# Depthwise and pointwise convolution in jobs of 784 pixels on four corners of the matrix engine, half of the ninth products summed by GpSimd, and a ratio by a scalar operand

## What is computed

```
x = x + L0(_gn(x))      # _gn: group norm over pairs of channels, eps 1e-5
x = x + L1(_gn(x))
L0(x): h = sign(x); h = depthwise 3x3 conv(h, sign(dw)); h = bn1(prelu(h)); h = sign(h)
       h = einsum('bchw,oc->bohw', h, sign(pw)); h = bn2(prelu(h)); return h + x
L1(x): filters = einsum('bchw,oc->bohw', x, W) + b        # 9 filter planes per channel
       return sum over the 9 taps k of (x shifted by tap k) * filters_k
```

## Time and profile before

| what | value |
|---|---|
| median of 3 runs | 834.75 us |
| the profiled execution | 835.78 us |
| its span, first to last instruction | 833.9 us |
| busy: VectorE (DVE) | 747.3 us, 90% |
| busy: TensorE (PE) | 702.7 us, 84% |
| busy: GpSimd (POOL) | 573.4 us, 69% |
| busy: ScalarE (ACT) | 518.5 us, 62% |

### The profile page before, as it was taken

One profiled execution on the slowest core, in us unless ns is written; L12 is line 12 of the kernel. 1 busy time (PEld: TensorE's weight loads), 2 busy tenths in 40 slices (PEclk: granted clock), 3 DMA queues, 4 the chain that ended last, 5 costly groups with the idle time before them and its releaser, 6 DMA issues.

```text
span 833.9 us, 19099 instructions
## 1 busy us (share of the span) xinstructions
PE 702.7 (84%) x7975; PEld 404.2 (48%) x7975; DVE 747.3 (90%) x1136; ACT 518.5 (62%) x772; POOL 573.4 (69%) x393
## 2 busy tenths in 40 slices
PE   0766889899998989998999989998999989897783
PEld 0323556455555555554555555554555555552221
DVE  6211799999999999999999999999999999999998
ACT  4586876667676767667685767766675767633000
POOL 2000167878787787878687786878787777778885
PEclk9988999999999999999999999999999999999986
DMA  5101559798887979698888889697988888686983
GB/s 205 44 1 31 140 115 248 149 210 192 173 219 160 235 147 246 139 233 170 210 182 173 215 163 247 140 238 159 217 180 171 212 172 165 142 174 143 198 165 95
DMA packets 40023, 142.14 MB, mean 170 GB/s; under 512 B 5248, under 2 KB 13440, under 8 KB 37888
## 3 DMA queue, kind: packets, MB, share of 16 engines
q0 software_dynamic: 17296, 75.87, 50.7%
q1 hardware_dynamic: 22640, 65.04, 23.4%
HBM read 25.86 MB, written 25.69 MB: 62 GB/s over the span
## 4 chain that ended last, share of the span: by engine, by line
DVE 56%; PE 32%; issue 6%; ACT 5%; DMA 1%; SPq 0%; DVEq 0%
DVE prod L685 35%; PE tap_ps L356 18%; PE dw_ps L369 11%; DVE prod L697 7%; DVE tap_ps L685 6%; DVE xb L659 4%; PE pw_ps L390 2%; ACT ab L416 2%; DVE st L651 1%; ACT unused L416 1%; PE pw_ps L381 1%; DVE st L555 1%; DMA prod<-prod 1%; ACT signs L416 1%; DVE prod L705 0%
## 5 line engine op out<-in xcount | busy, mean ns | idle before, releaser
L356 PE MATMUL tap_ps<-q,w_t 64*64 64x392 f32 x2304 | 466.9, 500 | 63.6 <-DVE prod L697 61.3
L356 PE MATMUL tap_ps<-mirror,w_t 64*64 64x392 f32 x2304 | 479.9, 517 | 0.0
L685 DVE SCALAR_TENSOR_TENSOR prod<-tap_ps,bias,q 128x784 f32<-128x784 f32 x448 | 452.3, 1029 | 11.5 <-PE tap_ps L356 7.3
L369 PE MATMUL dw_ps<-signs,dw_diag 64*64 64x392 bf16 x2304 | 246.3, 335 | 16.0 <-ACT ab L416 13.6
L416 ACT ACTIVATE ab<-dw_ps,col 128x392 bf16<-128x392 f32 x256 | 158.5, 669 | 160.0 <-PE dw_ps L369 160.0
L356 PEld LDWEIGHTS tap_ps<-q,w_t 64*64 64x64 f32 x2304 | 171.8, 134 | 166.9 <-DVE prod L697 95.8
L369 PEld LDWEIGHTS dw_ps<-signs,dw_diag 64*64 64x64 bf16 x2304 | 146.3, 108 | 139.2 <-issue 81.4
L282 POOL TENSOR_TENSOR prod<-prod 128x784 f32<-128x784 f32 x63 | 117.0, 1857 | 90.3 <-DVE prod L697 90.3
L289 POOL TENSOR_TENSOR prod<-prod 128x784 f32<-128x784 f32 x63 | 139.7, 2218 | 27.6 <-DMA prod<-prod 27.6
L356 PEld LDWEIGHTS tap_ps<-mirror,w_t 64*64 64x64 f32 x2304 | 124.6, 133 | 2.2
L304 POOL TENSOR_TENSOR ob<-prod 128x784 f32<-128x784 f32 x63 | 116.8, 1854 | 10.6 <-POOL prod L295 10.3
(11 more groups left out here) (101 smaller groups left out, 464.2 us busy)
## 6 DMA issues: line engine op xcount, KB each, us to landing
prod<-prod POOLq DMA_DIRECT2D x63, 1176.0 KB, 10.3
xb<-in_x_dram SPq DMA_DIRECT2D x16, 1568.0 KB, 11.7
out_dram<-ob SPq DMA_DIRECT2D x64, 392.0 KB, 2.9
mirror<-q SPq DMA_DIRECT2D x128, 101.5 KB, 4.6
prod<-prod SPq DMA_DIRECT2D x1, 146.2 KB, 2.3
prod<-in_L_conv_W_dram SPq DMA_DIRECT2D x1, 144.0 KB, 6.3
prod<-prod SPq DMA_DIRECT2D x1, 20.8 KB, 6.1
prod<-in_L_conv_prelu_a_dram SPq DMA_DIRECT2D x1, 0.2 KB, 2.3
```

The costliest lines, as they stand in the source:

```text
L356: mm = pe.matmul(rows3(tap_ps[to, u % SLOTS, side, 0:CH]), w_t[own, k, :], moving, start=True, stop=True)
L369: mm = pe.matmul(rows3(dw_ps[own, 0:CH]), dw_diag[own, k, own], signs[own, c * ROWS + dy:c * ROWS + dy + ROWS, dx:dx + WD], start=(k == 0) ...
L685: v.scalar_tensor_tensor(place.rearrange("p j (a b) -> p j a b", b=WD), psum.rearrange("p j (a b) -> p j a b", b=WD), s_(t, B4) if k == 4 ...
```

## The change

- L0 goes in 4 jobs of 784 pixels instead of 8 chunks of 392. `depthwise` has 36 matmuls a job, on all four corners: a corner's input rows are the image, its output columns the chunk. Signs, ReLU and `x1_sum` take 784 elements in one instruction. One buffer `conv_ps` (two banks) serves the depthwise result and then the pointwise one, so the next job's `depthwise` waits for this job's `x1_sum`. Jobs start at 20 + 9j.
- In odd quarters the ninth product is written to a ninth plane; there `pair` is left out. ScalarE adds the mean to that plane (`add_mean`) and GpSimd adds it (`add68`).
- `ratio` uses `tensor_scalar` with a per-partition scalar in place of `tensor_tensor`.
- x is kept in 3 buffers instead of 4, `signs` in 2 instead of 1. Many positions are moved.

```diff
-        xb = sb("xb", [P, RING, NPIX], F32)
-        signs = sb("signs", [P, HP, WP], BF16)
+        xb = sb("xb", [P, X_RING, NPIX], F32)          # X_RING = 3
+        signs = sb("signs", [P, 2, HP, WP], BF16)
-        dw_ps = ctx.enter_context(nc.psum_tensor("dw_ps", [P, 512], F32))
-        pw_ps = ctx.enter_context(nc.psum_tensor("pw_ps", [P, 512], F32))
+        conv_ps = ctx.enter_context(nc.psum_tensor("conv_ps", [P, 2, 512], F32))
+        def on_pool(g):
+            return g % 2 == 1
-                    wait(sp, q_done, load.count(2, -6))
+                    wait(sp, q_done, load.count(2, -4))
                 # add67
+                if on_pool(g):
+                    pool.wait_ge(prod_done, KK * g + 8)
+                    pool.tensor_tensor(pr[6], pr[6], pr[7], ALU.add).then_inc(summed67_first, 1)
+                else:
+                    pool.wait_ge(paired, g // 2 + 1)
+                    pool.tensor_tensor(pr[6], pr[6], pr[7], ALU.add).then_inc(summed67, 1)
+            def add68(t, qq):
+                if on_pool(g):
+                    pool.wait_ge(summed67_first, g // 2 + 1)
+                    pool.wait_ge(mean_added, g // 2 + 1)
+                    pool.tensor_tensor(pr[6], pr[6], pr[8], ALU.add).then_inc(summed67, 1)
                 # unit
-                if before % KK == PAIR_K:
-                    wait(pe, paired, before // KK + 1)
+                if before % KK == PAIR_K and not on_pool(before // KK):
+                    wait(pe, paired, before // KK // 2 + 1)
                 # depthwise
-                    wait(pe, ab_done, t.count(CHUNKS, c))
+                    wait(pe, x1_done, t.count(JOBS, j))
-                    for side in range(2):
-                        own = slice(side * C, side * C + C)
-                        mm = pe.matmul(rows3(dw_ps[own, 0:CH]), dw_diag[own, k, own], ...
+                    for image in range(2):
+                        own = slice(image * C, image * C + C)
+                        for chunk in range(2):
+                            to = slice(chunk * C, chunk * C + C)
+                            first = (2 * j + chunk) * ROWS + dy
+                            mm = pe.matmul(rows3(conv_ps[to, image, 0:CH]), dw_diag[own, k, own], ...
                 # step of TensorE; pointwise and add_h have the same four corners, 8 matmuls each
+                    for part in range(3):
+                        for t, j in jobs_due(u, part, mid, front):
+                            depthwise(t, j, range(3 * part, 3 * part + 3))
+            def conv_act(t, j):
+                act.wait_ge(dw_ready, t.count(JOBS, j + 1))
+                acts(ab[:, 0, :, :], conv_ps[:, :, 0:CH], ACT.Sign, scale=c_(A_SC), bias=c_(A_BI))
+                acts(ab[:, 1, :, :], conv_ps[:, :, 0:CH], ACT.Sign, scale=c_(B_SC), bias=c_(B_BI)).then_inc(ab_done, 1)
+            def add_mean(t, qq):
+                g = quarter(t, qq)
+                if on_pool(g):
+                    act.wait_ge(prod_done, KK * (g + 1))
+                    acts(prod[:, g % BUFS, 8, :], prod[:, g % BUFS, 8, :], ACT.Identity, bias=s_(t, MEAN1)).then_inc(mean_added, 1)
-                v.tensor_tensor(s_(t, RATIO), s_(t, INVZ), c_(S2_SG), ALU.mult).then_inc(ratio_done, 1)
+                v.tensor_scalar(s_(t, RATIO), s_(t, INVZ), c_(S2_SG), None, ALU.mult).then_inc(ratio_done, 1)
                 # x1_sum
+                xj = xb[:, t.x_slot, j * QP:(j + 1) * QP].rearrange("p (a n) -> p a n", a=2)
+                v.scalar_tensor_tensor(xj, conv_ps[:, :, 0:CH], s_(t, RATIO), xj, ALU.mult, ALU.add,
+                                       accum_out=sums[:, t.par, j:j + 1]).then_inc(x1_done, 1)
                 # last_quarter
-                v.tensor_tensor(pr[:, 0:2, :], pr[:, 0:2, :], pr[:, 6:8, :], ALU.add).then_inc(last_summed, 1)
+                dve.wait_ge(mean_added, g // 2 + 1)
+                v.tensor_tensor(pr[:, 0:3, :], pr[:, 0:3, :], pr[:, 6:9, :], ALU.add).then_inc(last_summed, 1)
-FIRST_CHUNK = 13, CHUNK_EVERY = 4, AB_DELAY = 2, PW_DELAY = 6, ADD_H_DELAY = 8, X1_DELAY = 9
+FIRST_JOB = 20, JOB_EVERY = 9, AB_DELAY = 3, PW_DELAY = 5, RELU_DELAY = 6, ADD_H_DELAY = 7, X1_DELAY = 5
-SUM0_AT = 1, MEAN0_AT = 1, SQUARE0_AT = 5, VAR0_AT = 7, R0_AT = 9, SIGN0_AT = 9, SCALES0_AT = 14
+SUM0_AT = 0, MEAN0_AT = 2, SQUARE0_AT = 9, VAR0_AT = 11, R0_AT = 13, SIGN0_AT = 9, SCALES0_AT = 18
-SUM1_AT = 18, MEAN1_AT = 15, SQUARE1_AT = 18, VAR1_AT = 21, R1_AT = 23, Q_AT = (23, 26)
+SUM1_AT = 19, MEAN1_AT = 18, SQUARE1_AT = 20, VAR1_AT = 21, R1_AT = 22, Q_AT = (27, 28)
+ADD68_DELAY = 14, MEAN_DELAY = 11
```

More of the change, by code:

```diff
@@ L15 @@
 RING = 4
+X_RING = 3
 EPS = 1e-5
@@ L307, in step @@
                 for u in range(UNITS):
-                    for what, delay in ((fold, FOLD_DELAY), (add67, ADD67_DELAY), (add45, ADD45_DELAY), (add36, ADD36_DELAY),
+                    for what, delay in ((fold, FOLD_DELAY), (add67, ADD67_DELAY), (add68, ADD68_DELAY), (add45, ADD45_DELAY), (add36, ADD36_DELAY),
                                         (final, OUT_DELAY)):
@@ L372, in depthwise, with pointwise @@
                 if taps.stop == KK:
                     mm.then_inc(dw_ready, 1)
-            def pointwise(t, c):
-                pe.wait_ge(ab_done, t.count(CHUNKS, c + 1))
-                wait(pe, x1_done, t.count(CHUNKS, c))
+            def pointwise(t, j):
+                pe.wait_ge(ab_done, t.count(JOBS, j + 1))
                 for n, pw_n in enumerate((pw_a, pw_b)):
-                    for side in range(2):
-                        own = slice(side * C, side * C + C)
-                        mm = pe.matmul(pw_ps[own, 0:CH], pw_n[own, own], ab[own, c % 2, n, :], start=(n == 0), stop=(n == 1))
+                    for chunk in range(2):
+                        own = slice(chunk * C, chunk * C + C)
+                        for image in range(2):
+                            to = slice(image * C, image * C + C)
+                            mm = pe.matmul(conv_ps[to, chunk, 0:CH], pw_n[own, own], ab[own, n, image, :],
+                                           start=(n == 0), stop=(n == 1))
@@ L382, in pointwise, with add_h @@
                 mm.then_inc(pw_ready, 1)
-            def add_h(t, c):
-                pe.wait_ge(relu_done, t.count(CHUNKS, c + 1))
+            def add_h(t, j):
+                pe.wait_ge(relu_done, t.count(JOBS, j + 1))
                 for n, pw_n in enumerate((pw_a_sg, pw_b_sg)):
[L388 to L391, removed]
+                    for chunk in range(2):
+                        own = slice(chunk * C, chunk * C + C)
+                        for image in range(2):
+                            to = slice(image * C, image * C + C)
+                            mm = pe.matmul(conv_ps[to, chunk, 0:CH], pw_n[own, own], ab[own, n, image, :],
+                                           start=False, stop=(n == 1), skip_group_check=True)
@@ L401, in step @@
                         unit(taps, u)
[L402 to L409, removed]
+                    for part in range(3):
+                        for t, j in jobs_due(u, part, mid, front):
+                            depthwise(t, j, range(3 * part, 3 * part + 3))
+                    for t, j in jobs_due(u, PW_DELAY, mid, front):
+                        pointwise(t, j)
+                    for t, j in jobs_due(u, ADD_H_DELAY, mid, front):
+                        add_h(t, j)
             program(step)
```

153 lines of the change are left out of this document (77 added, 76 removed).

## The result

The changed kernel takes 919.71 us in the median (918.24 to 920.77, 4 runs), the kernel before 835.3: the ratio is 1.1005, with a 95% interval of 1.0975 to 1.1034. The prediction was 872, with a range of 826 to 905. The direction and the waits came as described; what one term of the sum priced, the drops of TensorE's clock, cost about twice what I had put down. The profiled execution took 919.14 us, its span is 917.3, so the two spans differ by 83.4 us.

What follows compares the result with a forecast made beforehand. VectorE was taken as the bound, TensorE close behind. A step's 40.3 of work + 5.6 + 0.75 + 1.3 gave 48.0, with drops 50.0 against 46.4; with start and end +38.8 on 835.78, so 872 us, range 826 to 905.

Steps and rivals of the forecast that it cites:

- first product: At the start: 6 jobs instead of 14 chunks precede the first product, so it comes near 78, -10.5 us (-4 to -13).
- x1_sum's wait, a step: VectorE has nothing it may do before each x1_sum until a unit and add_h end: 1.40 us a job, 5.6 a step.
- var1's wait, a step: At the shuffle var1, three products instead of six cover the wait for square1: 0.75 us a step (0 to 1.8).
- after pairs and clock, a step: Behind pairs, units carrying thirds of the convolution cost VectorE 1.3 us a step; TensorE's lower clock adds 2.0.
- one of the 14 steps: A step carrying L0 and taps together: 48.0 us, 50.0 with the clock drops, against 46.4 before.
- step 14: The step with two jobs and no more: 44.6 us after 42.7 before, +1.9.
- last step and end: Two pairs and half of the drops fewer, a larger last sum (+0.8), GpSimd slightly late: -3 us.
- I take 2.5 drops a step, 2.0 us: TensorE's clock falls after idle times in the new steps, 0.8 us each time; bounds 0 and 5 us a step.
- the drops fall on the convolution: Rival: clock drops hit the convolution after a pair, costing 5 us a step instead of 2: 914 us; 12 in 100.
- The clock holds: Rival: TensorE keeps full clock while the waits stay, a step of 48.0 us: 843 us; 14 in 100.
- A relieved TensorE takes the loss after pairs away: Rival: no loss behind pairs and the clock holds, a step of 46.7 us: 825 us; 15 in 100.
- x1_sum doesn't wait: Rival: no wait before x1_sum, VectorE's removed work shows in full, a step of 42 us: 760 us; 4 in 100.

Runs made afterwards that it cites:

- Experiment 1: The changed kernel with x1_sum two positions later (X1_DELAY 7 for 5), so that it stands behind add_h as before: 819.22 us, ratio 0.9783.
- Experiment 2: The changed kernel with 2460 more instructions, matmuls that no one reads, in TensorE's idle times around the unit after x1_sum: 861.28 us, ratio 1.0292.
- experiment 6: The kernel before with the ratio by tensor_scalar, the ninth product on GpSimd and ScalarE in odd quarters, and x in 3 buffers: 838.04 us, ratio 1.003.
- experiment 7: The changed kernel with X1_DELAY 7 and the depthwise products in two parts (six taps, three taps), each ahead of its unit: 805.9 us, ratio 0.9637.

## Why the prediction was wrong, step by step

| step of the prediction | predicted | measured |
|---|---|---|
| first product | 78.1 (-10.5) | 78.78 (-9.84) |
| x1_sum's wait, a step | 5.6 | 5.9 idle, 6.2 with the lost overlap |
| var1's wait, a step | 0.75 | 8.6 / 14 = 0.6 |
| after pairs and clock, a step | 1.3 + 2.0 = 3.3 | 52.95 - 40.3 - 6.2 - 0.7 = 5.75 |
| one of the 14 steps | 50.0 | (820.14 - 78.78) / 14 = 52.95 |
| step 14 | +1.9 | 46.6 for 42.7, +3.9 |
| last step and end | -3 | 50.6 for 52.9, -2.4 |
| sum | +38.8 | +83.4 in the span |

**Right:** the start; the wait before each x1_sum, with its price and its number (56 in 14 steps); the wait at var1; the ratio; VectorE's busy share (78% said, 75%). Experiment 1 shows the order that makes this wait as the cause of the loss: moving x1_sum alone takes 100 us off.

**The step that failed** is the price in "I take 2.5 drops a step, 2.0 us": 0.8 for a drop. The mechanism was right and so was the number of drops, 35 in 14 steps, though that was a guess between none and four and partly luck: I had not foreseen steps with two and with three. The price was about half of the true one. Experiment 2, where the drops are gone, separates it: 3.9 us a step, so 1.5 a drop, where I had 2.0 and 0.8. The loss after pairs without a drop was right (1.5 a step there for 1.3). In the changed kernel both together are 5.75 us a step instead of 3.3, which is 34 of the 44 us that were missing in the sum.

I took 0.8 from the last tile, where no convolution follows the pair and TensorE has slack to make good the slower units. Even there it was too little: the tile has three drops (windows 792 to 800, 804 to 808 and 812 to 820), and the clock stays at 1.00 behind the first pair (780 to 792), so the 3.3 us are 1.1 a drop. In the steps the drop comes where three units each carry a third of a convolution. There it costs, with the loss after the pair, 3.2 us behind each pair of the 53.7 us step (416.84 - 408.77, less five operations of 0.945 and the shuffle's 0.1), 2.0 and 2.3 in the 52.1 us step (363.49 - 356.64 and 390.54 - 383.45, the same way) and some 0.5 in its job without a pair (12.67 us from x1_sum to x1_sum, 12.14 without a drop). That makes 6.4 and 4.8, on the mean 5.6 beside the 5.75 of the table, so the 40.3 for the work stands. My own rival "the drops fall on the convolution" (914, given 12 in 100) had the right place and too high a price, 5 us a step: the measured 3.9 lies between it and the forecast. The time is above even its 914, because the small terms below lie on the same side.

The rest is small: the x1 wait was 0.6 a step longer, some 8 us in all, and step 14 lost 2.0 more than I had.

**The rivals.** "The clock holds" (843) is what experiment 2 made, 861 with its filler matmuls. "A relieved TensorE takes the loss after pairs away" (825) fell: TensorE's busy time fell by 45 us, and products waited for it more. "x1_sum doesn't wait" (760) fell too; even experiment 1, which takes that wait away, stays at 819, with a step of 45.87, so a step of 42 was not reached even without it.

**The ratio.** The row shows 0.20 us, and in experiment 6 the operation at 392.21 took 0.21 while a GpSimd add ran (392.05, 2.23 long). So one element with a scalar operand didn't stand for GpSimd. I had read only half of the Trainium skill's page "SBUF — State Buffer", section "Who interferes with whom". Its rule on tensor_scalar holds for a two-port mode, whose condition, as the prediction has it, one element doesn't meet. The same section says that a VectorE instruction with two inputs in SBUF contends with a GpSimd instruction that reads SBUF, and that one with at most one such input, outside the two-port modes, doesn't. The rows agree with both: 1.72 us for the tensor_tensor, 0.21 for the tensor_scalar.

**The clock.** What decides on a drop stays open. Each of the 28 pairs of the 14 steps, with two holes and one unit between them (2.10 and 1.93 at 407.02 and 409.85), came with a drop; of the 28 jobs without a pair, with one hole of about 2.1, 7 did, one in every second step; the kernel before dropped behind single holes of 1.94 (before 792.58, window 792 to 796 at 0.68). The Trainium skill's page "TensorE: Matmul & The Clock Gate", section "HAM oscillation — how this bites in real kernels", describes a loop whose array starts cold after every pause, but each of those pauses is a wait for a DMA of some 3 to 5 us. The changed kernel's holes between 80 and 820 are 2.17 us at most, so the case described there is another, and it couldn't have told me how many of mine bring a drop.

**What the parts are worth.** Put right, with the convolution ahead of its unit, the 784-pixel jobs and the ratio are worth 33 us together (801.2 for 834.2), of which the ratio alone gave 15 on the kernel before. The GpSimd part gave nothing in either form in which it was measured: +17 us on the kernel before, 4.7 us less without it in the last form, where the two intervals overlap. What holds the form of experiment 7 at 806 is open: taking away its var1 wait or most of its mirror wait changed nothing.

## What to carry to other kernels

Two engines that each work through a list in order need distance between a result and its use: count, for every wait, what the other engine may still do while it lasts. A wait that leaves both with nothing costs its full chain, here 1.4 us for each job, and with the clock more. Price a clock drop where the work behind it is dense, not where there is slack, and count the drops in more than one step, since two steps that look alike can differ; before work is taken from TensorE, look at the holes in its timeline that would grow together. And an operation taken from the bounding engine is worth nothing until the engines that get it have been checked for what stands behind it in their order.

## What the hardware showed beyond that

- More matmuls made a kernel faster: 2460 useless ones took 920 us to 861.
- Four matmuls of 64 rows on four corners took 0.17 us in full clock (add_h starts its first four at 404.42 and its second at 404.59), as long as two on two corners.
- Large sums on VectorE beside a GpSimd add stretch both. In the changed kernel's end, VectorE and then GpSimd:

```profile
906.84 4.12 DVE L741 TENSOR_TENSOR prod<-prod 128x2352 f32<-128x2352 f32 x1
910.99 2.49 DVE L743 TENSOR_TENSOR prod<-prod 128x784 f32<-128x784 f32 x1
913.51 0.97 DVE L746 TENSOR_TENSOR ob<-prod 128x784 f32<-128x784 f32 x1
```

```profile
904.30 4.20 POOL L312 TENSOR_TENSOR prod<-prod 128x784 f32<-128x784 f32 x1
908.66 3.99 POOL L321 TENSOR_TENSOR ob<-prod 128x784 f32<-128x784 f32 x1 [0.17 <-POOL prod L312]
```

A sum of 784 takes 2.49 us beside a GpSimd add and 0.97 without, and the adds, 1.9 us elsewhere, take 4.
